# Sorting graph edges in a four-layer graph network: one-hot products on TensorE in place of indexed scatters

## The reference

```python
edge_index = jnp.stack([src, dst])
h = jnp.maximum(_layernorm(x, axis=-1), 0.0)
x = x + _L0_gnn_ref(h, edge_index, ...)
...
def gnn_layer(x, W, b, src, dst):
    h = x @ W.T + b
    msgs = h[src]
    agg = jax.ops.segment_sum(msgs, dst, num_segments=N_NODES)
    return jax.nn.relu(agg)
```

## Time and profile before

| | us |
|---|---|
| median of 3 runs | 2798.69 (2797.72 to 2799.21) |
| the profiled execution | 2799.54 |
| its span in the profile | 2797.8 |
| TensorE busy in the span | 2459.9 (88%) |
| VectorE busy | 2024.5 (72%) |
| ScalarE busy | 1373.6 (49%) |
| GpSimd busy | 1709.9 (61%) |
| mean granted TensorE clock | 0.982 of full speed |

### The profile page before, as it was taken

How to read it: one execution, slowest core, us unless ns; L and a number is a source line. 1 busy time by engine, 2 the same in 40 slices (tenths; PEclk the granted TensorE clock), 3 DMA queues, 4 the chain that set the end, 5 groups by cost and what they waited for, 6 DMA issues and landing times. The chain is left out here.

```text
span 2797.8 us, 46999 instructions
## 1 busy us (share of the span) xinstructions
PE 2459.9 (88%) x13660; PEld 2095.8 (75%) x13660; DVE 2024.5 (72%) x5281; ACT 1373.6 (49%) x2875; POOL 1709.9 (61%) x1832
## 2 busy tenths in 40 slices
PE   3555379998988886999999969999999699999998
PEld 3344268887877776999999958888888588888886
DVE  7777666664655554888877869999999666666666
ACT  1555334454776764555555523333333245555553
POOL 0565345554566765777777647777777445555553
PEclk9999999999999998999999989999999799999999
DMA  8677643533444543343333333333334245555553
GB/s 246 206 209 206 196 125 113 146 119 114 127 134 145 156 151 127 111 129 115 113 118 114 107 110 123 114 115 114 116 120 121 85 139 153 153 153 153 153 152 110
DMA packets 145287, 385.55 MB, mean 138 GB/s; under 512 B 34127, under 2 KB 34287, under 8 KB 144554
## 3 DMA queue, kind: packets, MB, share of 16 engines
q0 software_dynamic: 100144, 300.93, 36.0%
q1 hardware_dynamic: 45002, 83.04, 9.5%
HBM read 259.61 MB, written 148.26 MB: 146 GB/s over the span
## 5 line engine op out<-in xcount | busy, mean ns | idle before, releaser
L1830 ACT CAST d_Thi<-d_pt 128x512 fp32r<-128x512 f32 x79 | 46.4, 587 | 307.8 <-DVE d_pt L787 276.7
L1678 PE MATMUL c_pu<-c_Zhi,parts 128*128 128x256 f32 x640 | 182.0, 284 | 5.3 <-DVE c_Zlo L1596 5.3
L1680 PE MATMUL c_pu<-c_Zhi,parts 128*128 128x256 f32 x640 | 181.8, 284 | 0.0
L1679 PE MATMUL c_pu<-c_Zlo,parts 128*128 128x256 f32 x640 | 180.6, 282 | 0.0
L815 POOL DMA_INDIRECT f_Gsrc<-rows,indexS x79 | 76.0, 962 | 170.4 <-PE f_phsrc L2159 161.4
L2075 ACT ACTIVATE f_Mhi<-f_pm 128x512 fp32r<-128x512 f32 x79 | 47.3, 598 | 262.2 <-DVE f_pm L2108 255.6
L2099 DVE TENSOR_TENSOR f_Hlosrc<-f_phsrc,f_Hhisrc 128x512 fp32r<-128x512 f32 x79 | 54.6, 692 | 159.6 <-ACT f_Hhisrc L2069 127.7
L794 PE MATMUL b_po<-parts,b_Thi 128*128 128x512 f32 x316 | 132.4, 419 | 41.0 <-issue 26.1
L819 POOL DMA_INDIRECT h<-a_rows,indexD x79 | 79.6, 1008 | 117.7 <-ACT a_rows L1172 109.0
L1565 ACT ACTIVATE c_pu<-c_pu,c_b1col 128x256 f32<-128x256 f32 x160 | 61.6, 448 | 167.6 <-PE c_pu L1680 167.6
L794 PE MATMUL d_po<-parts,d_Hhi 128*128 128x512 f32 x316 | 131.2, 415 | 1.9 <-DVE d_Hlo L1848 1.9
(11 more groups left out here) (451 smaller groups left out, 9548.0 us busy)
## 6 DMA issues: line engine op xcount, KB each, us to landing
rows<-r_xt SPq DMA_DIRECT2D x40, 520.0 KB
h<-q_zerorow SPq DMA_DIRECT2D x80, 256.0 KB
r_xt<-in_x SPq DMA_DIRECT2D x80, 256.0 KB
a_wstage<-in_L_W SPq DMA_DIRECT2D x3, 1024.0 KB
selrowsD<-selD SPq DMA_DIRECT2D x1, 2640.0 KB
selrowsS<-selS SPq DMA_DIRECT2D x1, 2640.0 KB
q_keyrowD<-in_dst POOLq DMA_DIRECT2D x1, 2560.0 KB, 17.0
q_keyrowS<-in_src POOLq DMA_DIRECT2D x1, 2560.0 KB
```

What stands on the lines that cost most here:

```text
L1678: pe.matmul(psum_u[:, o, :], g.Whi[2][:, c, cols], Zhi[:, c, :], start=c == 0, stop=False)
L1679: pe.matmul(psum_u[:, o, :], g.Whi[2][:, c, cols], Zlo[:, c, :], start=False, stop=False)
L1680: ins = pe.matmul(psum_u[:, o, :], g.Wlo[2][:, c, cols], Zhi[:, c, :], start=False, stop=c == C - 1)
```

## The change

The sorted edges are no longer scattered to memory and loaded back. They are built in two PSUM banks, `psort`, 80 rows of 128 places: for each tile and each key one fp32 product of `hot_hi` (128 edges x 80, one-hot of the position's high part) and `values` (128 edges x 256: the one-hot of the position's low part, times key + 1 in the left half and times the other end in the right half). The product accumulates over all 79 tiles.

- `pick` writes the position itself; the count of earlier equal keys is added by TensorE in the same bank (128 columns instead of 1), and the position instructions go. Every eight tiles (then 4, then 3) VectorE splits eight positions into high and low part (`split`, four instructions).
- GpSimd makes `hot_hi` of D and `values` of both keys for tiles 0 to 75, five instructions a tile (`make`); VectorE makes all of these for tiles 76 to 78 behind its loop. ScalarE makes `hot_hi` of S for all tiles (`hot_column`), 11 tiles behind its own loop.
- TensorE's `sort(T-12)` stands behind `look(T)` in its stream. The rings of `hot_hi` and `values` are 3 deep.
- The owner stage reads `psort` directly. The neighbour keys come from two tiny products each.
- The counting block works on 79 tiles instead of 80, `count` is cleared first, and the sentinel rows go with their six transfers.

```diff
-    g.sorted = {k: nc.dram_tensor("edges" + k, [N + 3 * P, 4], F32, kind="Internal").ap() for k in KEYS}
...
-        totals = sb("totals", [NT, P], F32)
-        sentinel = sb("sentinel", [P, 4], F32)
+        totals, down = sb("totals", [NT, P], F32), sb("down", [NT, NT], F32)
+        psort = {k: ps("psort" + k, [P, 512]) for k in KEYS}
...
+        hot_hi = {k: first.ring("hothi" + k, SLOTS, [P, NT], F32) for k in KEYS}
+        values = {k: first.ring("values" + k, SLOTS, [P, 2 * P], F32) for k in KEYS}
+        key_up = {k: first.sb("keyup" + k, [P, NT], F32) for k in KEYS}
+        hi_square = first.sb("hisquare", [P, NT], F32)
...
-                with dve.Fori(0, NT // HOT) as group:
-                    some = bass.ds(group * HOT, HOT)
+                for k in KEYS:
+                    dve.tensor_scalar(key_up[k][:, :], key_f[k][:, :], 1.0, None, ALU.add)
+                dve.tensor_scalar(down[:, :], g.iota_f[0:NT, 0:NT], g.pidx[0:NT, 0:1], 1.0, ALU.subtract, ALU.is_equal)
...
+                with dve.Fori(0, ET // HOT) as group:
+                    one_hot(bass.ds(group * HOT, HOT), HOT)
+                with dve.Fori(0, 2) as part:
+                    dve.wait_ge(s_one, part + ET // HOT)
+                    one_hot(bass.ds(part * (HOT // 2 - 1) + ET // HOT * HOT, HOT // 2), HOT // 2)
...
+            EACH = 8
+            LATE = (ET - 1) // 4 * 4
+            SPLITS = [(first, EACH) for first in range(0, LATE - 4, EACH)] + [(LATE - 4, 4), (LATE, ET - LATE)]
+            place, place_i, part_i = (f.sb(n, [P, 3, 2, EACH], dt) for n, dt in
+                                      (("place", F32), ("placei", I32), ("parti", I32)))
+            hi_part, lo_part = f.sb("hipart", [P, 3, 2, EACH], F32), f.sb("lopart", [P, 3, 2, EACH], F32)
...
+            def make(eng, T, k, hi, signal):
+                m, s, one = KEYS.index(k), T.slot(SLOTS), slice(T.t, T.t + 1)
+                half, j = column(T)
+                wait(eng, q_sorted[k], T.t - SLOTS + 1)
+                lo = lo_part[:, half, m, j:j + 1]
+                if hi:
+                    eng.tensor_scalar(hot_hi[k][s][:, :], g.iota_f[:, 0:NT], hi_part[:, half, m, j:j + 1], None, ALU.is_equal)
+                eng.tensor_scalar(values[k][s][:, 0:P], g.iota_f[:, :], lo, key_up[k][:, one], ALU.is_equal, ALU.mult)
+                eng.tensor_scalar(values[k][s][:, P:2 * P], g.iota_f[:, :], lo, key_f[OTHER[k]][:, one],
+                                  ALU.is_equal, ALU.mult).then_inc(signal, 1)
...
-                for k in KEYS:
-                    for row, n in ((P - 1, 1), ((ET + 1) * P, (NT - ET) * P), (N + P, 1)):
-                        sp.dma_start(g.sorted[k][row:row + n, :], sentinel[0:n, :]).then_inc(q_end, 16)
...
                 def pick(T):
-                    s, r = T.slot(2), T.slot(R)
-                    for k in KEYS:
+                    s = T.slot(2)
+                    half, j = column(T)
+                    for m, k in enumerate(KEYS):
                         dve.wait_ge(q_look[k], T.t + 1)
                         dve.scalar_tensor_tensor(picked[k][:, :], plook[k][s][:, 0:P], 1.0, OHlo[k][:, bass.ds(T.t, 1), :],
-                                                 ALU.mult, ALU.mult, accum_out=posf[k][s][:, :])\
+                                                 ALU.mult, ALU.mult, accum_out=place[:, half, m, j:j + 1])\
                             .then_inc(q_pick[k], 1)
+                def split(n):
...
+                    dve.tensor_copy(whole_i, whole).then_inc(q_part, 1)
+                    dve.wait_ge(q_part, 3 * n + 1)
+                    dve.tensor_scalar(upper, whole_i, 7, None, ALU.logical_shift_right).then_inc(q_part, 1)
+                    dve.wait_ge(q_part, 3 * n + 2)
+                    dve.tensor_copy(hi, upper).then_inc(q_part, 1)
+                    dve.wait_ge(q_part, 3 * n + 3)
+                    dve.scalar_tensor_tensor(lo, hi, float(-P), whole, ALU.mult, ALU.add).then_inc(q_split, 1)
...
+                        for n, (first, size) in enumerate(SPLITS):
+                            if i * RX + u == first + size - 1:
+                                split(n)
+                dve.wait_ge(q_const, 1)
                 straight(NT // RX, 1, 1, body)
+                dve.wait_ge(q_split, len(SPLITS))
+                for t in range(LATE, ET):
+                    for k in KEYS:
+                        make(dve, Tile(0, t, ET), k, k == "D", q_late[k])
...
-                def move(T):
-                    r = T.slot(R)
-                    for k in KEYS:
-                        pool.wait_ge(q_pos[k], T.t + 1)
-                        pool.wait_ge(q_ends[k], T.t + 1)
-                        pool.sem_inc(q_tick, 1)
-                        pool.indirect_dma_start(g.sorted[k], bass.IndirectOffsetOnAxis(ap=posi[k][r][:, 0:1], axis=0),
-                                                cargo[k][r][:, :], None).then_inc(q_moved[k][r], 16)
...
+                for t in range(LATE):
+                    T = Tile(0, t, ET)
+                    pool.wait_ge(q_split, group(T) + 1)
+                    for k in KEYS:
+                        make(pool, T, k, k == "D", q_made[k])
...
-                def name_ends(T):
-                    r = T.slot(R)
-                    for m, k in enumerate(KEYS):
-                        wait(act, q_moved[k][r], 16 * T.use(R))
-                        act.sem_inc(q_tick, 1)
-                        nc.scalar.copy(cargo[k][r][:, 0:2], ends[:, bass.ds(T.t, 1), m:m + 2]).then_inc(q_ends[k], 1)
+                def hot_column(T):
+                    half, j = column(T)
+                    act.wait_ge(q_split, group(T) + 1)
+                    wait(act, q_hihot, T.t)
+                    nc.scalar.activation(hi_square[:, :], g.iota_f[:, 0:NT], ACT.Square, bias=hi_part[:, half, 1, j:j + 1],
+                                         scale=-1.0).then_inc(q_hisquare, 1)
+                    act.wait_ge(q_hisquare, T.t + 1)
+                    wait(act, q_sorted["S"], T.t - SLOTS + 1)
+                    nc.scalar.activation(hot_hi["S"][T.slot(SLOTS)][:, :], hi_square[:, :], ACT.Relu, bias=ones_f[:, 0:1],
+                                         scale=-1.0).then_inc(q_hihot, 1)
...
                         at(i, u, 1, U, ET, hot)
-                        at(i, u, 0, U, ET, name_ends)
+                        at(i, u, -11, U, ET, hot_column)
...
                         pe.wait_ge(q_hot[k], T.t + 1)
-                        wait(pe, q_pos[k], T.t - 1)
-                        pe.matmul(plook[k][s][:, 0:P], OHhiT[k][s][:, :], table[k][s][:, :], start=True, stop=True)
+                        wait(pe, q_pick[k], T.t - 1)
+                        pe.matmul(plook[k][s][:, 0:P], OHhiT[k][s][:, :], table[k][s][:, :], start=True, stop=False)
                         pe.wait_ge(q_early[k], T.t + 1)
-                        pe.matmul(plook[k][s][:, P:P + 1], earlier[k][s][:, :], ones_b[:, 0:1],
-                                  start=True, stop=True, skip_group_check=True).then_inc(q_look[k], 1)
+                        pe.matmul(plook[k][s][:, 0:P], earlier[k][s][:, :], ones_b[:, :],
+                                  start=False, stop=True).then_inc(q_look[k], 1)
...
+                def sort(T):
+                    s = T.slot(SLOTS)
+                    for k in KEYS:
+                        if T.t < LATE:
+                            pe.wait_ge(q_made[k], T.t + 1)
+                        else:
+                            pe.wait_ge(q_late[k], T.t - LATE + 1)
+                        if k == "S":
+                            pe.wait_ge(q_hihot, T.t + 1)
+                        pe.matmul(psort[k][0:NT, 0:2 * P], hot_hi[k][s][:, :], values[k][s][:, :], start=T.t == 0, stop=T.t == ET - 1,
+                                  skip_group_check=True).then_inc(q_sorted[k], 1)
                 def body(i):
                     for u in range(U):
                         at(i, u, 0, U, ET, look)
-                straight(GR, 0, 0, body)
+                        at(i, u, -12, U, ET, sort)
+                straight(GR, 0, 2, body)
...
+                for k in KEYS:
+                    step(dve.tensor_copy(rowT[k][:, 1:P + 1], psort[k][0:NT, 0:P]), "key" + k)
                 for m, k in enumerate(KEYS):
-                    dve.wait_ge(o_ld[k], 48)
+                    dve.wait_ge(o_next, m + 1)
+                    step(dve.tensor_copy(rowT[k][:, 0:P + 2:P + 1], plast[k][0:NT, 300:302]))
...
-                    step(dve.tensor_copy(key, record[k][:, :, 0]))
...
-                    step(dve.tensor_copy(scol[k][:, 0:2, :], ptr[k][:, 0:2 * NT]))
+                    step(dve.tensor_scalar(scol[k][:, 0, :], ptr[k][:, 0:NT], -1.0, None, ALU.add))
+                    step(dve.tensor_copy(scol[k][:, 1, :], ptr[k][:, NT:2 * NT]))
...
             def _(act):
+                for k in KEYS:
+                    act.wait_ge(o_v, marks["key" + k])
```

(54 more changed lines are left out.)

69 lines of the change are left out of this document (28 added, 41 removed).

## The result

The changed kernel takes 2842.36 us (median of 4 runs, 2840.56 to 2844.09) against 2798.95 for the kernel before (4 runs): ratio 1.0154, interval 1.0137 to 1.0172. It is 1.5% slower, where 0.4% faster was forecast, and above the upper end of the range, 2828. On chip 11 both kernels were run again: 2808.48 against 2725.18, ratio 1.0303 (1.0286 to 1.032). The kernel before is 74 us faster there, the changed one 34. In the four sets of experiments the kernel before took 2724.20, 2725.18, 2725.75 and 2725.47 us (chips 3, 11, 11 and 12), so runs of different sets can be compared to about 2 us.

What follows compares the result with a forecast made beforehand. VectorE and its fourth-tile wait were taken to set the sort loop. Loop -13.7, start -2, drain +4.6 and owner stage -1.3 sum to -12.4 us against 2799.5: 2787.1, or 2786.3 as median; range 2758 to 2828.

Steps and rivals of the forecast that it cites:

- GpSimd's price: Sort loop: GpSimd's five new instructions take 1.8 us a tile (1.0 to 2.3), hidden below VectorE's 3.03.
- Rival D: Sort loop: GpSimd is the bound, above 0.6 us an instruction; at 0.7, +35 us in all, 2834; chance 0.10.
- Loop: Sort loop over the tiles: 3.03 us a tile instead of 3.21, 76 x -0.18 = -13.7 us.
- VectorE's 3.03: VectorE's time a tile in the sort loop: 2.59 us by itself plus 0.44 for the shared port.
- TensorE's 2.97: TensorE's time a tile in the sort loop: 1.67 + 0.1 + 1.2 = 2.97 us (2.6 to 3.3).
- The port's 0.44 us: Sort loop: GpSimd reading SBUF delays four two-input VectorE instructions a tile by 0.11 us each, 0.44 in all.
- Both signs: Sort loop: prediction wrong if picks are spaced above 3.2 us, or if GpSimd is the engine others wait for.
- The likeliest case: Whole kernel: the forecast's own case, chance 0.42, said to span 2775 to 2800 us with TensorE at 2.8 to 3.2.
- the fourth-tile wait: Sort loop: every fourth tile VectorE's pick of S starts 1.55 us late, 28.9 us in all; assumed to go.
- Drain: Last look-up to owner stage: seven unsorted tiles left for GpSimd, 18.0 us instead of 13.4, +4.6 us.
- Start: Kernel start: six sentinel transfers no longer precede the loads of x, so VectorE's first statistics come earlier, -2 us.
- Owner stage: After the sort: 2.70 us of loads and a copy go, products and copies come, -1.3 us.

Runs made afterwards that it cites:

- gp_four: Changed kernel with one of GpSimd's five instructions a tile left out, so part of the result is missing: 2753.13 us, ratio 1.011 to the kernel before.
- narrow_sort: Changed kernel with TensorE's sort products cut from 256 to 128 columns after the first tile, GpSimd's work kept, result incomplete: 2806.93 us.

## Why the prediction was wrong

**The step that failed** is GpSimd's price: "The nearest is the 128x128 select with one input, 328 ns: 4 x 0.33 + 0.28 = 1.6, with 0.2 for the shared port 1.8 us (1.0 to 2.3). Below 3.03, so hidden in the loop." It measured 0.81 to 0.85 us for each of four and 0.50 for the fifth, 3.70 a tile. The upper bound had no room for it, because it was taken from an operation of another form: a cheap one on this engine, 0.45 us for 128 columns with two inputs, where the comparison and multiplication by two scalars takes 0.78. Rival D, "GpSimd is the bound", is what happened; it named the point (0.6 us an instruction) and gave 2834 at 0.7, but held a chance of 0.10 and lay outside the range. That "even its two-input addition scales to 0.46" was no argument against it: two inputs aren't the dearest form. The page "GPSIMD Engine Reference" of the Trainium skill, section "4.1 Engine selection", says of GpSimd beside VectorE that "1-input is roughly line-rate". Read as VectorE's rate, by its 0.34 to 0.36 us for the same 128-column instruction in this trace (tiles 76 to 78) and 0.39 for the 80-column one, that would be 1.8 us a tile, and the trace does not agree.

**Loop**, forecast -13.7, measured +19.0: the same step. The terms beneath it were nearer. VectorE's 3.03 and TensorE's 2.97 were both too high: where GpSimd has four instructions (gp_four) the pace is 2.78 with all of TensorE's products. The port's 0.44 us was mis-sized: the two comparisons went from 332 and 345 ns to 348 and 375, 46 ns together, and the norm's two-input steps from about 0.16 to 0.2 us; 0.1 to 0.15 us a tile. TensorE's products started 0.43 us apart in a dense stream, and in the loop it waited for GpSimd, never the other way round; narrow_sort shows that their size costs nothing. The sum took TensorE's prices from rows at the full clock and had no term for its fall to 0.60 to 0.77 in the loop; behind GpSimd that cost nothing, which is luck and not foresight.

Both signs that were to show the prediction wrong came: the picks are 3.46 us apart, above 3.2, and GpSimd is the engine that others wait for. Two readings in it are off without bearing on this. The likeliest case "spans 2775 to 2800", but TensorE at 2.8 gives 2769 by the same sum, or 2786 with VectorE at 3.03 binding. And 0.32 us idle is what stands before the scatter of S; before that of D it is 81.7 / 79 = 1.03.

**The base of the comparison.** "This takes it that the fourth-tile wait goes": the late pick of S went (idle before it 10.1 us instead of 28.9), but only because a longer wait came before it, that for D's look-up. On chip 11 it is not there to begin with, and 3.21 is 2.70. At that pace even the forecast's 3.03 would have lost some 25 us. The 83 us of loss on chip 11 and the 43 on the first differ by this alone, within 2 us: the changed kernel's sort ends within 1.7 us of the same moment on both.

**Drain**, from the last look-up to the owner block: forecast 18.0, measured 375.95 - 336.60 = 39.35. GpSimd has nine tiles left then, 67 to 75, from 337.77 to 370.42: 3.63 each instead of 1.8, and 5.5 us of products and barrier follow. The seven tiles were off too, since an engine that is itself the bound doesn't get its three slots ahead.

**Start**, forecast -2, measured -1.4 on the first chip but -0.1 on chip 11; in the changed kernel's variants the pick of tile 2 stands anywhere from 73.69 to 74.95, so the term is small and its mechanism not shown. **Owner stage**, forecast -1.3, measured 1.13 - 3.02 = -1.9: right in mechanism and near in size. That "the later layers neither gain nor lose" was right within 2 us.

## What to carry to other kernels

Work given to an engine that has never done it in the trace has no upper bound from rows of other forms: measure one instruction of the very form before the sum, or leave the range open on that side, above all where the price is multiplied by hundreds and an in-order engine waits for each. Before work is moved off a busy engine, look at where that engine waits for its own last result: an instruction that needs nothing new, put into such a gap, was free here (2.52 instead of 2.70 us a tile), and taking one out of a gap cost more than it saved (2.92). And where a stage's pace rests on a wait that no releaser explains, the sum should also be made without that wait.

## What the hardware showed unexpectedly

The same program ran the sort loop at 3.21 us a tile on one chip and at 2.70 on another, with every VectorE instruction as long as before, and the layers in 2428 and 2393 us; what makes the difference is open. TensorE's granted clock was lower in the run with the narrower products (0.50 from 200 to 250 us) than with the full ones (0.61 on chip 11, 0.77 on the first chip), and at 1.00 in gp_four with the full products at a quicker pace; between the 1.2 and 2.4 GHz levels, then, half the columns at the same pace got the lower one. In the kernel before, with TensorE busy only 27 to 29 of 50 us from 100 to 300 us, it stayed at 1.00. What decides is open.
